# A Perceiver's local attention: the softmax of two batches at once, and the outputs joined one pair later

## The reference, cut to what matters

```python
q = norm(x) @ Wq.T + bq                     # 16 heads of 16
pos = reference + q @ Woff.T + boff         # 5 positions a head and token, scaled and wrapped
k, v = ctx @ Wk.T + bk, ctx @ Wv.T + bv
K[n] = interpolate(k, pos[n])               # between two neighbouring keys, zero outside
V[n] = interpolate(v, pos[n])
w = softmax(q . K[n] / sqrt(16), over the 5 positions)
x = x + concat(sum_n w[n] * V[n]) @ Wo.T + bo
```

## Time and profile before

| | us |
|---|---|
| median of 3 runs (2602.79 to 2608.9) | 2605.1 |
| the profiled execution, its own time | 2597.09 |
| its span | 2595.2 |
| PE busy in the span | 2339.2 (90%) |
| DVE busy | 1332.0 (51%) |
| ACT busy | 957.5 (37%) |
| POOL busy | 886.5 (34%) |
| mean granted TensorE clock, share of full | 0.937 |

### The profile page before, as it was taken

The page is one execution under the profiler, slowest core; times in us unless marked ns, Lnnn a source line. Parts: engine busy times, 40 slices in busy tenths (PEclk is TensorE's granted clock), DMA queues, the critical chain, the costliest instruction groups (busy, mean ns, idle before and its releaser), DMA issues. The chain is left out here.

```text
span 2595.2 us, 35945 instructions
## 1 busy us (share of the span) xinstructions
PE 2339.2 (90%) x13845; PEld 1829.4 (70%) x13845; DVE 1332.0 (51%) x2478; ACT 957.5 (37%) x2031; POOL 886.5 (34%) x534
## 2 busy tenths in 40 slices
PE   3787759949999999999999999999999997687897
PEld 2454445647888888888888888888888885234684
DVE  3897533343544544544544544544544444796554
ACT  1564121123433443443443443443433443442231
POOL 2563215225414314314214224224233100474355
PEclk8898869979999999999999999999999998787799
DMA  3100063121102102102102002101111004001264
GB/s 101 16 13 5 1 231 112 35 92 56 47 31 62 37 29 68 31 30 73 28 16 90 25 19 76 33 25 59 45 30 54 13 1 204 8 0 41 72 151 116
DMA packets 69927, 141.32 MB, mean 54 GB/s; under 512 B 24912, under 2 KB 42576, under 8 KB 65408
## 3 DMA queue, kind: packets, MB, share of 16 engines
q1 hardware_dynamic: 62992, 120.50, 14.6%
q0 software_dynamic: 6768, 18.49, 3.1%
HBM read 124.21 MB, written 14.75 MB: 54 GB/s over the span
## 5 line engine op out<-in xcount | busy, mean ns | idle before, releaser
L2182 PE MATMUL img_ps<-cn,pt_hi 127*128 127x512 f32 x1536 | 551.3, 400 | 10.1 <-POOL cn L1909 10.0
L2183 PE MATMUL img_ps<-cn,pt_lo 127*128 127x256 f32 x1536 | 430.7, 280 | 0.0
L1907 POOL TENSOR_SCALAR ct<-staged 128x762 fp32r<-128x762 f32 x64 | 136.1, 2126 | 757.6 <-DMA staged<-in_ctx_t 525.3
L2182 PEld LDWEIGHTS img_ps<-cn,pt_hi 127*128 127x128 f32 x1536 | 289.8, 189 | 69.6 <-POOL cn L1909 10.2
L2308 DVE TENSOR_TENSOR pt_lo<-t_ps,pt_hi 127x512 fp32r<-127x512 f32 x384 | 241.5, 684 | 138.6 <-ACT pt_hi L2302 138.6
L2159 PE MATMUL s_ps<-ct,a_hi 128*128 128x508 f32 x768 | 312.5, 407 | 0.0
L2160 PE MATMUL s_ps<-ct,a_hi 128*128 128x508 f32 x768 | 301.8, 393 | 0.0
L2161 PE MATMUL s_ps<-ct,a_lo 128*128 128x508 f32 x768 | 301.8, 393 | 0.0
L2183 PEld LDWEIGHTS img_ps<-cn,pt_lo 127*128 127x128 f32 x1536 | 289.7, 189 | 0.0
L2365 ACT ACTIVATE prob<-s_ps,bias 128x1524 f32<-128x1524 f32 x128 | 196.5, 1535 | 141.0 <-DVE bias L2421 140.9
L2302 ACT ACTIVATE pt_hi<-t_ps 127x512 fp32r<-127x512 f32 x384 | 202.1, 599 | 80.9 <-PE t_ps L2169 77.2
(11 more groups left out here) (367 smaller groups left out, 3994.9 us busy)
## 6 DMA issues: line engine op xcount, KB each, us to landing
staged<-in_ctx_n SPq DMA_DIRECT2D x64, 384.0 KB, 3.2
staged<-in_ctx_t SPq DMA_DIRECT2D x64, 381.0 KB, 3.2
up_all_m<-in_up SPq DMA_DIRECT2D x8, 2048.0 KB, 13.1
down_all_m<-in_down SPq DMA_DIRECT2D x8, 1024.0 KB, 23.7
sums_m<-y_b SPq DMA_DIRECT2D x63, 128.0 KB, 2.3
w_shared<-in_wq SPq DMA_DIRECT2D x7, 1024.0 KB, 5.7
w_shared<-in_wo SPq DMA_DIRECT2D x7, 1024.0 KB, 4.8
win<-in_ctx_near SPq DMA_DIRECT2D x16, 128.0 KB, 2.1
```

Source lines behind the costliest of these rows:

```text
L1907: nc.gpsimd.tensor_scalar(hi, piece, 1.0, None, ALU.mult).then_inc(first.hi_done, 1)
L2182: nc.tensor.matmul(img_ps[:], pt_hi[0:IBLK, j, :], rows[0:IBLK, :, j, :], start=j == 0, stop=False)
L2183: last = nc.tensor.matmul(img_ps[:, D:2 * D], pt_lo[0:IBLK, j, :], rows[0:IBLK, 0, j, :], start=False, stop=j == IB - 1)
```

## The change

- A pair of batches goes through the maximum, the difference, the exp, the total, the reciprocal and the weights in one set of operations on twice the width. Score, shifted, total, inverse and the three areas of `marks` double in size. `SOFT`, the count of the softmax's semaphore, is 7 a pair (two sums over keys and five steps) where it was 6 a batch.
- There are four tent buffers and four value buffers in place of two, and two share buffers in place of one. `qblk`, `kt`, `win`, `hit` and the PSUM tiles stay as they were.
- PE's order becomes, for a pair b, b+1: scores(b+1), keys_values(b+2), scores(b+2), keys_values(b+3), sums(b), turn_sums(b), sums(b+1), outputs(b), turn_sums(b+1), outputs(b+1).
- DVE's order becomes hits(b), keep_outputs(b-2), hits_summed(b), keep_outputs(b-1), hits(b+1), keep_values(b+2), hits_summed(b+1), the joined softmax, shares(b), keep_values(b+3), shares(b+1).
- ACT does the tents of three half parts (b+2, both, b+3, first) before the exp of the pair, and spread_sums with keep_turned of a batch one right after the other.
- POOL's `prepare` waits for the second set of positions from the second batch on; before, the first two batches waited for the first set only.

```diff
--- before
+++ after
-    vals = [sb(f"vals{s}", [P, D]) for s in range(2)]
+    vals = [sb(f"vals{s}", [P, D]) for s in range(4)]
     qblk = [sb(f"qblk{s}", [P, C, TILES0, 8, QT]) for s in range(2)]
-    tent = [sb(f"tent{s}", [P, NK, TILES0, QW]) for s in range(2)]
-    hit, share = sb("hit", [P, NK, TILES0, QW]), sb("share", [P, NK, TILES0, QW])
+    tent = [sb(f"tent{s}", [P, NK, TILES0, QW]) for s in range(4)]
+    hit, share = sb("hit", [P, NK, TILES0, QW]), [sb(f"share{s}", [P, NK, TILES0, QW]) for s in range(2)]
     spread = sb("spread0", [P, TILES0 * (WN + QT)])
-    score, shifted = sb("score", [P, PK]), sb("shifted", [P, PK])
+    score, shifted = sb("score", [P, 2, PK]), sb("shifted", [P, 2 * PK])
     turned = sb("turned0", [P, H0, S])
-    total = sb("total0", [P, TILES0])
-    inv = sb("inv0", [P, TILES0])
+    total = sb("total0", [P, 2 * TILES0])
+    inv = sb("inv0", [P, 2 * TILES0])
...
-    top, attn, weight = marks[:, 0:TILES0], marks[:, PK:2 * PK], marks[:, 2 * PK:3 * PK]
+    top, attn, weight = marks[:, 0:2 * TILES0], marks[:, 2 * PK:4 * PK], marks[:, 4 * PK:6 * PK]
...
-        for s in range(2):
-            keys_values(s, s, 0)
-            scores(s, s)
-        def body(i, first, last):
-            for s in range(2):
-                b = i * 2 + s
-                sums(b)
-                if not last:
-                    keys_values(b + 2, s, i + 1)
-                turn_sums(b)
-                if not last:
-                    scores(b + 2, s)
-                outputs(b, s)
-        pairs_of_batches(pe, body)
+        keys_values(0)
+        scores(0)
+        keys_values(1)
+        for b in range(0, NB, 2):
+            scores(b + 1)
+            if b + 2 < NB:
+                keys_values(b + 2)
+                scores(b + 2)
+                keys_values(b + 3)
+            sums(b)
+            turn_sums(b)
+            sums(b + 1)
+            outputs(b)
+            turn_sums(b + 1)
+            outputs(b + 1)
     @block.gpsimd
     def _(pool):
-        def prepare(b, s, old):
-            if old is not None:
-                pool.wait_ge(scored, old)
+        def prepare(b):
+            s = b % 2
+            if b >= 2:
+                pool.wait_ge(scored, b - 1)
...
             last.then_inc(q_masked, 1)
-            pool.wait_ge(k.pos_in[0 if old is None else 1], H0 * 16)
+            pool.wait_ge(k.pos_in[0 if b == 0 else 1], H0 * 16)
             for h in range(2):
-                if old is not None:
-                    pool.wait_ge(share_done, old * 2 + (h - 1))
+                if b >= 4:
+                    pool.wait_ge(share_done, (b - 4) * 2 + h + 1)
                 points = POINTS[h].stop - POINTS[h].start
                 nc.gpsimd.tensor_tensor(
-                    tent[s][:, POINTS[h]], small(k, "iota").rearrange("p (i m) -> p i m", m=QW)
+                    tent[b % 4][:, POINTS[h]], small(k, "iota").rearrange("p (i m) -> p i m", m=QW)
                     .unsqueeze(1).broadcast_to([P, points, TILES0, QW]),
...
-        prepare(0, 0, None)
-        def body(i, first, last):
-            for s in range(2):
-                b = i * 2 + s
-                if not (last and s == 1):
-                    prepare(b + 1, 1 - s, None if first and s == 0 else b)
-        pairs_of_batches(pool, body)
+        for b in range(NB):
+            prepare(b)
...
+        def keep_sums(b):
+            spread_sums(b)
+            for g in range(2):
+                keep_turned(b, g)
+        keep_keys(0)
         for h in range(2):
-            distances(0, 0, h)
-            tents(0, 0, h)
+            distances(0, h)
+            tents(0, h)
+        keep_keys(1)
         act.wait_ge(spread_zeroed, 1)
-        def body(i, first, last):
-            for s in range(2):
-                b = i * 2 + s
-                after, old = not (last and s == 1), not (first and s == 0)
-                if after:
-                    distances(b + 1, 1 - s, 0)
-                if old:
-                    spread_sums(b - 1)
-                if after:
-                    tents(b + 1, 1 - s, 0)
-                act.wait_ge(soft, b * SOFT + 3)
-                nc.scalar.activation(weight, shifted[:], ACT.Exp).then_inc(exp_done, 1)
-                if after:
-                    keep_keys(b + 1, 1 - s)
-                if old:
-                    for g in range(2):
-                        keep_turned(b - 1, g)
-                if after:
-                    distances(b + 1, 1 - s, 1)
-                    tents(b + 1, 1 - s, 1)
-        pairs_of_batches(act, body)
-        spread_sums(NB - 1)
-        for g in range(2):
-            keep_turned(NB - 1, g)
+        for h in range(2):
+            distances(1, h)
+            tents(1, h)
+        for b in range(0, NB, 2):
+            after = b + 2 < NB
+            if b:
+                keep_sums(b - 1)
+            if after:
+                distances(b + 2, 0)
+                tents(b + 2, 0)
+                keep_keys(b + 2)
+                distances(b + 2, 1)
+                tents(b + 2, 1)
+                distances(b + 3, 0)
+                tents(b + 3, 0)
+            act.wait_ge(soft, b // 2 * SOFT + 4)
+            nc.scalar.activation(weight, shifted[:], ACT.Exp).then_inc(exp_done, 1)
+            if after:
+                keep_keys(b + 3)
+                distances(b + 3, 1)
+                tents(b + 3, 1)
+            keep_sums(b)
+        keep_sums(NB - 1)
...
-        def keep_values(b, s):
-            if not isinstance(b, int) or b > 1:
-                dve.wait_ge(out_done, b - 1)
+        def keep_values(b):
+            if b >= 4:
+                dve.wait_ge(out_done, b - 3)
             dve.wait_ge(kv_done, b + 1)
-            nc.vector.tensor_tensor(vals[s][:], v_ps[:, 0:D], k.bias("bv0"), ALU.add).then_inc(v_kept, 1)
+            nc.vector.tensor_tensor(vals[b % 4][:], v_ps[:, 0:D], k.bias("bv0"), ALU.add).then_inc(v_kept, 1)
         def by_tile(ap):
-            return ap.unsqueeze(2).broadcast_to([P, TILES0, NK])
+            return ap.unsqueeze(2).broadcast_to([P, 2 * TILES0, NK])
         def tiled(ap):
             return ap.rearrange("p (a n) -> p a n", n=NK)
...
+        def hits(b):
+            dve.wait_ge(tent_step, b * 4 + 4)
+            dve.wait_ge(scored, b + 1)
+            if b:
+                dve.wait_ge(soft, b // 2 * SOFT + b % 2)
+            nc.vector.tensor_tensor(
...
+                ALU.mult).then_inc(hit_done, 1)
+        def hits_summed(b):
+            dve.wait_ge(hit_done, b + 1)
+            nc.vector.tensor_reduce(score[:, b % 2].rearrange("p (i n) -> p n i", n=NK), hit[:], AX,
+                                    ALU.add).then_inc(soft, 1)
+        def shares(b):
+            if b >= 2:
+                dve.wait_ge(summed, (b - 2) * 2 + 2)
+            for h in range(2):
+                points = POINTS[h].stop - POINTS[h].start
+                own = attn[:, b % 2 * PK:(b % 2 + 1) * PK]
+                nc.vector.tensor_tensor(share[b % 2][:, POINTS[h]], tent[b % 4][:, POINTS[h]],
+                                        tiled(own).rearrange("p i n -> p n i")[:, POINTS[h]].unsqueeze(3)
+                                        .broadcast_to([P, points, TILES0, QW]), ALU.mult).then_inc(share_done, 1)
         nc.vector.memset(spread[:], 0.0).then_inc(spread_zeroed, 1)
-        pairs_of_batches(dve, body)
-        keep_outputs(NB - 1)
+        keep_values(0)
+        keep_values(1)
+        for b in range(0, NB, 2):
+            at = b // 2 * SOFT
+            hits(b)
+            if b:
+                keep_outputs(b - 2)
+            hits_summed(b)
+            if b:
+                keep_outputs(b - 1)
+            hits(b + 1)
+            if b + 2 < NB:
+                keep_values(b + 2)
+            hits_summed(b + 1)
+            dve.wait_ge(soft, at + 2)
+            both = tiled(score[:].rearrange("p j a -> p (j a)"))
+            nc.vector.tensor_reduce(top, both, AX, ALU.max).then_inc(soft, 1)
+            dve.wait_ge(soft, at + 3)
+            nc.vector.tensor_tensor(tiled(shifted[:]), both, by_tile(top), ALU.subtract).then_inc(soft, 1)
+            dve.wait_ge(exp_done, b // 2 + 1)
+            nc.vector.tensor_reduce(total[:], tiled(weight), AX, ALU.add).then_inc(soft, 1)
+            dve.wait_ge(soft, at + 5)
+            nc.vector.reciprocal(inv[:], total[:]).then_inc(soft, 1)
+            dve.wait_ge(soft, at + 6)
+            nc.vector.scalar_tensor_tensor(out=tiled(attn), in0=tiled(weight), scalar=0.5, in1=by_tile(inv[:]),
+                                           op0=ALU.mult, op1=ALU.mult).then_inc(soft, 1)
+            dve.wait_ge(soft, at + 7)
+            shares(b)
+            if b + 2 < NB:
+                keep_values(b + 3)
+            shares(b + 1)
+        for b in (NB - 2, NB - 1):
+            keep_outputs(b)
```

More of the change, by code:

```diff
@@ L497, in near_attention @@
     block = ctx.enter_context(nc.Block())
-    def pairs_of_batches(eng, body):
-        for i in range(HALVES):
```

(27 more changed lines are left out.)

61 lines of the change are left out of this document (13 added, 48 removed).

## The result

The changed kernel takes 2684.35 us (median of 4 runs, 2677.58 to 2687.16) against 2605.23 before (4 runs): ratio 1.0285, 95% interval 1.0265 to 1.0304, which is 69 to 79 us slower. The forecast was 2673, in a range of 2653 to 2692.

What follows compares the result with a forecast made beforehand. DVE was taken to bound the steady part, with PE close behind. Pairs +32.0, start +13.8, end +5.7 and clock +16.4 gave +67.9 us on the median 2605.1: 2673, range 2653 to 2692.

Steps and rivals of the forecast that it cites:

- Small operations joined: DVE: softmax steps done once a pair save 1.2 us a pair, 10 us in all if DVE stays the bound.
- A steady pair: Batches A and B in the steady part: 27.5 us a pair at full clock, +32.0 us over six pairs.
- What holds the pair: On PE, outputs of A queue behind sums of B, so DVE's join of A has a new 5.2 us wait.
- rival d: Steady pair bound by DVE and the start hidden too, so only the operations are saved: 2595 us; chance 0.04.
- Start: Up to the third product: the second batch's tent waits for all positions, so that product comes 13.8 us later.
- rival (c): Steady pair bound by DVE at 20.6 us, only the late positions cost: +10.1 us, 2615; chance 0.03.
- End: From the fifteenth product to the stage's end: 38.1 us instead of 32.36, +5.7 us.
- The clock: PE: a 4.8 us hole in every pair drops the clock, costing sums of A 2.05 us, 16.4 in all.
- Rival (a): PE's clock holds through the hole in each pair: 2657 us; chance 0.2.
- rival (b): PE's clock falls twice a pair, at the hole and among the copies parting the transposes: 33 us, 2690; chance 0.1.
- Four tents: POOL: four tent buffers don't let it run ahead; queries for odd batches wait 12 us for scores.

Runs made afterwards that it cites:

- e7: Changed kernel with PE, DVE and ACT queues reordered and the second batch waiting for the first positions only: ratio to before 0.9970, steady pair 20.20 us.
- e8: e7 with the softmax of each batch done by its own operations on half the width: ratio to before 0.9979, steady pair 21.04 us.
- e3: Changed kernel with nine unused matmuls put into PE's hole ahead of a pair's first sums, in seven of eight pairs: ratio to before 1.0217.
- e2: Changed kernel with PE's outputs of a pair's first batch put ahead of the sums of the second: ratio to before 1.0326, pair 31.7 us.
- e4: Changed kernel with DVE's two joins of outputs moved behind the first two reductions over keys: ratio to before 1.0284, pair 30.2 us.
- e6: Changed kernel with PE's scores and following keys moved ahead of the sums of a pair's second batch: ratio to before 1.0284, pair 30.8 us.
- e5: Changed kernel with ACT's exp and key copy put ahead of its first tent passes of the fourth batch: ratio to before 1.0204, pair 28.0 us.
- e1: Changed kernel with the second batch's tent waiting for the positions of the first two batches alone: ratio to before 1.0260, third product at 99.5 us.
- e11: Changed kernel run again without edit, on the chip of the later comparison: ratio to before 1.0285, pair 30.2 us.

## Why the prediction was right, and where it was not

The result lies in the range, the sign and the mechanism of the steady pair hold. Step by step:

- **Small operations joined.** Mis-sized. The term was 1.2 us a pair; e7 against e8 measures 0.84. It had counted the exp's wait and every operation at its whole interval, and an operation with an independent neighbour costs less.
- **A steady pair.** The working gave 27.5 us at full clock with a join wait of 5.2; e3 shows 27.60 and 5.31. The exp's wait was put at 1.5 and measured 1.61, the wait for scores at 0.4 and measured 0.39. The rows of before were enough for this.
- **What holds the pair.** Here the prediction's reading of its own schedule was wrong. It called the wait of the join for the outputs of A the new wait, and let the other side (rival d) decide "from the point where the sums of B no longer stand ahead of the outputs of A". e2 moved exactly that and lost 11 us more; e4 took the join out of the way and nothing changed; e6 freed the scores and nothing was gained. The pair is held by a ring: shares of A, both sums, the copies of ACT between the transposes, outputs, the scores that stand last on PE, the product, keys, POOL's queries and tents, ACT's passes, exp, shares. The working of the prediction has this ring step by step; it was the conclusion drawn from it, that the sums of B ahead of the outputs of A decide, that was wrong. Taking the last link out (e5) gains; moving one inner link only moves the wait. The three orders together gave DVE its bound back (e7, 20.2 us); whether two of them would do was not tried.
- **Start.** +13.8 forecast, +15.9 measured; the positions landed 2.1 us later than in the profile of before (80.20 for 78.07), which is the difference: from the landing the working gave 26.3 us to the third product, and it is 26.2. But rival (c) gave the whole to the late positions, and e1 gives their wait 6.7; of the rest e5 gives 4.2 to ACT's passes ahead of the first exp, which stood in the working and not in its conclusion.
- **End.** 38.1 us of full clock, 43.7 measured with two falls of 3.03 and 2.11 us: 38.5 without them.
- **The clock.** That each hole makes the first sums slow was right: eight holes, eight slow sums. The price was put at 2.05 us, from two falls; the mean of the eight is 2.26. Rival (a), that the clock holds, is refuted; e3 measures what it would have given. The sum had put the second fall of rival (b), among the copies that part the transposes, at nothing. It comes in two of the six pairs of the changed kernel (the scores of 1.98 us at 119.71 and 149.93) and costs 1.3 and 1.1 us there: the six pairs, less 27.60 and less what the first sums ahead of each lose, leave 1.3, 1.1, 0.0, 0.0, 0.0 and 0.0. Rival (b) had put it at 1.3 us in every pair; in e6 scores are slow in every pair.
- **Four tents.** That they don't let POOL run ahead was right: its queries wait 14.66 us, where 12 was forecast.

The forecast fell 11 us short of the median: 7.3 in the stage (the falls in the first sums 1.7, the landing 2.1, the second falls 2.4, the pair at full clock 0.6 over six, the end 0.4), the rest in the part of the program that the change doesn't touch, where executions differ by more than that. So the number rests on a working that held at full clock to 0.1 us a pair, and on a price of the clock that came near with one kind of fall left out.

What stays open: why a fall costs from 1.60 to 3.03 us behind holes of the same 4.7 us (1.35 behind the first, of 3.63). The sequence of lengths (5.91, 6.16, 6.23, 7.09, 7.37, 7.51, 7.59) is the same in e1 and the changed kernel, and stands shifted in e4 and e11, so it isn't noise; I did not try what sets it.

## What to carry to other kernels

Work out the schedule of in-order queues before moving an operation, and then ask of each wait whether the chain changes if it goes: a wait that is long on the busiest engine may be only the place where the ring shows. When two batches are processed at once, ask of every queue whether its order interleaves them; here joining the arithmetic while PE, ACT and POOL still take one batch after the other opened a hole of 5 us in each pair that the joined operations, worth 0.84 us, could never pay. The hole of 4.7 us on PE cost twice here, once as time and once as a lower clock on the work behind it. And before two starts are compared, look at when the data they wait for landed: here it moved by 5 us between executions, as much as some of the effects looked for.

## What the runs showed of the hardware

- Nine matmuls whose result nobody reads, put into the hole, made the program 18 us faster (e3), with the first sums at 4.53 us instead of 5.9 to 7.6. A hole of 3.4 us was followed by a slow sum in four of six pairs (e5), and holes of 1.29 us (e8) and 0.46 us (e7) in none of the steady pairs. One of 2.2 us was followed by a slow sum in every pair of e6, but there a hole of 3.67 us and slow scores stand just ahead of it. So the length of the last hole alone doesn't decide.
- DVE: two dependent small operations start 0.22 to 0.24 us apart, two independent ones 0.11 (e8). The Trainium skill (VectorE: DVE Perf Modes, The DRAIN you can't avoid) says that dropping the waits between chained operations gains nothing, and also that a next operation that is not held starts earlier. The trace agrees with the second sentence, 0.11 against 0.24, in all eight pairs of e8.
- Doubling the width from 40 to 80 elements cost 0.03 to 0.05 us an operation (0.24 or 0.25 for 0.20), as the slope of the large operations had given.
